# Extra products of the identity on TensorE in the waits at the beginnings and ends of stages

## The reference

```python
x = x + L0_xattn(ln(x), ctx, ctx)      # l0a: 16 heads, softmax over 256 keys
x = x + L0_ffn(ln(x))                  # l0f: mixture of experts, 1 of 8 experts for a token
x = x + L1_xattn(ctx, ln(x))           # dtw: dynamic time warping alignment
x = x + L1_ffn(ln(x))                  # l1f: silu(gate) * up, down
x = x + L2_xattn(ln(x), ctx)           # l2a: attention with rotated q and k
x = x + L2_ffn(ln(x))                  # l2f: mixture of experts, 2 of 8 for a token
x = x + L3_xattn(ln(x), ctx, ctx)      # l3a: attention over the 32 largest scores
x = x + L3_ffn(ln(x))                  # l3g finds token groups, l3f attends within them
```

## Time and profile before

| | us |
|---|---|
| median of 3 runs | 2589.59 (2580.96 to 2591.77) |
| the profiled execution, its own time | 2591.72 |
| its span, first to last instruction | 2589.9 |
| mean granted clock of TensorE | 0.790 of full speed |
| busy: PE, DVE, ACT, POOL | 2011.9, 1664.3, 1115.9, 1012.3 |

### The profile page before, as it was taken

The page is one execution under the profiler, slowest core; times in us unless marked ns, Lnnn a source line. Parts: engine busy times, 40 slices in busy tenths (PEclk is TensorE's granted clock), DMA queues, the critical chain, the costliest instruction groups (busy, mean ns, idle before and its releaser), DMA issues. The chain is left out here.

```text
span 2589.9 us, 40039 instructions
## 1 busy us (share of the span) xinstructions
PE 2011.9 (78%) x13073; PEld 1624.0 (63%) x13073; DVE 1664.3 (64%) x5395; ACT 1115.9 (43%) x3119; POOL 1012.3 (39%) x955
## 2 busy tenths in 40 slices
PE   6985898699559948866999847777777778765996
PEld 4664797699538835555999835555555555544663
DVE  5764111588972258843111189999999999964773
ACT  3552232555221114431333246666666666641443
POOL 3310453200000046403555446666666666606430
PEclk9996899655779979967999966667667666567997
DMA  2111575410210012124464230000000000000112
GB/s 88 65 55 58 215 244 182 121 21 1 81 37 1 0 45 73 57 69 145 136 212 156 80 96 9 1 9 9 1 9 9 1 1 1 1 7 26 42 47 77
DMA packets 91587, 161.09 MB, mean 62 GB/s; under 512 B 18366, under 2 KB 69718, under 8 KB 83414
## 3 DMA queue, kind: packets, MB, share of 16 engines
q0 software_dynamic: 23808, 85.50, 9.6%
q1 hardware_dynamic: 67576, 73.06, 9.0%
HBM read 194.38 MB, written 33.33 MB: 88 GB/s over the span
## 5 line engine op out<-in xcount | busy, mean ns | idle before, releaser
L555 DVE MATCH_REPLACE8 l3a_left<-l3a_top,l3a_left 128x256 f32<-128x256 f32 x768 | 308.9, 410 | 0.0
L548 DVE MAX8 l3a_top<-l3a_left 128x8 f32<-128x256 f32 x768 | 286.0, 415 | 0.0
L365 POOL TENSOR_TENSOR l3a_prob<-l3a_expd,l3a_rest 128x512 f32<-128x512 f32 x128 | 162.5, 1270 | 230.3 <-ACT l3a_rest L445 230.0
L270 PE MATMUL l3a_psT<-all_ident,l3a_prob 128*128 128x128 f32 x512 | 123.5, 387 | 163.9 <-POOL l3a_prob L365 163.9
L288 PE MATMUL l3a_psO<-l3a_probT,l3a_vp 128*128 128x128 f32 x1024 | 216.0, 377 | 28.8 <-ACT l3a_probT L461 28.8
L288 PEld LDWEIGHTS l3a_psO<-l3a_probT,l3a_vp 128*128 128x128 f32 x1024 | 185.5, 271 | 81.7 <-ACT l3a_probT L461 48.3
L270 PEld LDWEIGHTS l3a_psT<-all_ident,l3a_prob 128*128 128x128 f32 x512 | 83.8, 196 | 186.6 <-POOL l3a_prob L365 186.1
L352 POOL TENSOR_TENSOR l3a_kept<-l3a_raw_sc,l3a_mone 128x512 f32<-128x512 f32 x128 | 163.3, 1276 | 49.1 <-ACT l3a_raw_sc L429 48.9
L1465 ACT ACTIVATE l2f_hT<-l2f_psH,l2f_wt 128x128 f32<-128x128 f32 x312 | 89.2, 369 | 216.3 <-PE l2f_psH L1397 216.3
L445 ACT ACTIVATE l3a_rest<-l3a_left,l3a_nmax 128x256 f32<-128x256 f32 x256 | 116.1, 502 | 151.5 <-DVE l3a_left L555 150.8
L932 POOL TENSOR_SCALAR l2a_xn<-all_x,l2a_nmean,all_rstd 128x256 f32<-128x256 f32 x16 | 8.8, 562 | 433.6 <-DVE all_rstd L106 433.6
(11 more groups left out here) (528 smaller groups left out, 4715.5 us busy)
## 6 DMA issues: line engine op xcount, KB each, us to landing
o_at<-l0a_oraw SPq DMA_DIRECT2D x16, 256.0 KB, 2.0
l0a_osum<-o_at SPq DMA_DIRECT2D x32, 128.0 KB
kv_at<-dtw_kv SPq DMA_DIRECT2D x8, 512.0 KB, 2.8
o_at<-l2a_oraw SPq DMA_DIRECT2D x16, 256.0 KB, 2.0
l2a_osum<-o_at SPq DMA_DIRECT2D x32, 128.0 KB
l2f_yb<-rows_y SPq DMA_DIRECT2D x8, 512.0 KB, 7.4
o_at<-l3f_oraw SPq DMA_DIRECT2D x16, 256.0 KB, 2.0
l3f_osum<-o_at SPq DMA_DIRECT2D x32, 128.0 KB
```

The source lines that it names most:

```text
L270: mm = nc.tensor.transpose(psT[u % 2][:, kc, e, :], prob[:, u % 4, e, kc * P:kc * P + P], ident[:])
L365: nc.gpsimd.tensor_tensor(prob[:, u % 4, :, :], expd[:, u % 2, :, :], rest[:, u % 2, :, :], ALU.subtract).then_inc(picked, 1)
L548: ins = nc.vector.max(top[:, e, eight], rows[:, e, :] if r else scores[:, e, :])
L555: ins = nc.vector.match_replace(out=rows[:, e, :], in_to_replace=top[:, e, eight], in_values=rows[:, e, :] if r else scores[:, e, :], imm_ ...
```

## The change

A new helper issues `n` products of the 128 x 128 identity with four copies of itself side by side (512 columns) into a PSUM bank, which the next real product overwrites; nothing reads them and they signal nothing. It is called in four functions, always just before a wait of TensorE: in `paired_attention` before the first `x_norm` (2), before the first `xT_ev` (2), before `scores_1(0)` waits (11 in l2a, 3 in l3f, none in l0a), before `values(15)` (1) and before `out_project(7)` (8); in `moe` before `turn(0)` (4); in `gated_ffn` at the start (2) and after the first transpositions (1); in `find_groups` at the start (1) and before `queries(0)` (3). In `scores_1` the four `take`s also move ahead of the two other waits.

```diff
--- before.py
+++ after.py
@@ -72,6 +72,13 @@
 
     def block(self):
         return self.blocks.enter_context(self.nc.Block())
+
+
+def keep_busy(nc, out, ident, n):
+
+
+    for _ in range(n):
+        nc.tensor.matmul(out, ident[:], ident[:].unsqueeze(1).to_broadcast([P, 4, P]), start=True, stop=True)
 
 
 class RowStats:
@@ -766,8 +773,13 @@
                     mm = nc.tensor.matmul(out, lhs[c], rhs[c], start=(c == 0), stop=(c == DC - 1))
                 return mm
 
+            def busy(out, n):
+                keep_busy(nc, out[:].rearrange("p e n -> p (e n)"), ident, n)
+
             def x_turned(b):
                 out = take("xT", b)
+                if b == 0:
+                    busy(out, 2)
                 pe.wait_ge(x_norm, b + 1)
                 for c in range(DC):
                     for t in range(QT):
@@ -776,6 +788,8 @@
 
             def projected(b, what):
                 out = take(what, b)
+                if b == 0 and what == "q":
+                    busy(out, 2)
                 if what == "q" or not given:
                     pe.wait_ge(xT_ev, b + 1)
                 else:
@@ -792,10 +806,14 @@
 
             def scores_1(n):
                 b, c, qt = n // 4, n % 4 // 2, n % 2
+                out = [take("s1", 4 * n + j) for j in range(4)]
+                if n == 0 and groups is not None:
+                    busy(out[0], 3)
+                if n == 0 and rope is not None:
+                    busy(out[0], 11)
                 if n % 4 == 0:
                     pe.wait_ge(qd_set, b + 1)
                     pe.wait_ge(k2_set, b + 1)
-                out = [take("s1", 4 * n + j) for j in range(4)]
                 for e in (1, 0):
                     for j in range(4):
                         r = slice(32 * j, 32 * j + 32)
@@ -828,6 +846,8 @@
             def values(y):
                 b, c = y // 2, y % 2
                 out = take("pv", y)
+                if y == 2 * B - 1:
+                    busy(out, 1)
                 pe.wait_ge(exp_done, 8 * (y + 1))
                 if c == 0:
                     pe.wait_ge(v_ev, b + 1)
@@ -841,6 +861,8 @@
 
             def out_project(b):
                 out = take("out", b)
+                if b == B - 1:
+                    busy(out, 8)
                 if groups is None:
                     pe.wait_ge(o_set, 2 * (b + 1))
                 else:
@@ -1436,6 +1458,7 @@
                                       start=(n == 0), stop=(n == KT - 1))
             mm.then_inc(turned, 1)
 
+            keep_busy(nc, psX[:], ident, 4)
             turn(0)
             up(0)
             turn(1)
@@ -2104,6 +2127,8 @@
                     for t in range(QT):
                         mm = nc.tensor.transpose(psT[:, c * S + t * P:c * S + t * P + P], xn[:, p, t, c * P:c * P + P], ident[:])
                 mm.then_inc(t_done, 1)
+                if not again:
+                    keep_busy(nc, psG[0][:], ident, 1)
                 pe.wait_ge(t_read, b + 1)
                 if not again:
                     pe.wait_ge(w_set, 1)
@@ -2128,6 +2153,7 @@
                                               start=(f == 0), stop=(f == HC - 1))
                 mm.then_inc(y_ps, 1)
 
+            keep_busy(nc, psG[0][:], ident, 2)
             pe.wait_ge(x_norm, 1)
             up(0, 0, False)
             up(1, 1, True)
@@ -2288,11 +2314,14 @@
                                               start=(c == 0), stop=(c == DC - 1))
                 mm.then_inc(q_ps, 1)
 
+            keep_busy(nc, psQ[0][:].rearrange("p t n -> p (t n)"), ident, 1)
             turn(0)
             pe.wait_ge(w_in, 48)
             for b in range(B):
                 if b + 1 < B:
                     turn(b + 1)
+                if b == 0:
+                    keep_busy(nc, psQ[0][:].rearrange("p t n -> p (t n)"), ident, 3)
                 queries(b)
             pe.wait_ge(c_done, 1)
             nc.tensor.transpose(psF[0:4 * NT, :], col[:].rearrange("p f t -> p (f t)"), ident[:]).then_inc(f_done, 1)
```

## The result

The changed kernel takes 2575.0 us (median of 12 runs, 2559.6 to 2582.4) against 2585.7 us for the kernel before beside it (12 runs, 2579.3 to 2591.8): 10.7 us less, a ratio of 0.9947 with a 95% interval of 0.9932 to 0.9962 (the two medians by themselves give 0.9959). The forecast was 2576, faster. Three executions of this document's kernels lie far above all others of their kernel (5936.0 and 4485.1 us of the kernel before, 2834.5 of the kernel with calls in the body), and no median counts them.

The account below looks back on a forecast made before the run. TensorE's low clock after idle waits was taken to bound stretches where others wait for it. Ten terms sum to 14.2 us (best 22.4, worst about -5): 2577.5 from the profile, 2575.4 on the median's scale, forecast 2576, range 2566 to 2590.

Parts of the forecast that it names:

- l0a beginning: Start of l0a: four calls keep TensorE dense before q, so q and k run fast; gain 2.3 us (0 to 3.1).
- l3f end: End of l3f: eight calls overrun 4.07 us of idle, out_project(7) starts 2.7 to 4.2 late; -1.2 us (-2.4 to -0.9).
- l2f: Expert block l2f: four calls before turn(0) end 0 to 1.6 late, up(0) 3.73 for 6.73; 2.1 us (-0.1 to 3.1).
- l0f: Expert block l0f: calls end before the gather lands, clock probably falls again; 0.6 us (0 to 1.9).
- l1f: l1f: three calls at the start and behind the transpositions, L2118's first eight could win 1.8; 0.9 us (-0.2 to 2.0).
- l2a beginning: Start of l2a: faster q 1.6, eleven calls before scores_1(0) perhaps 2.1 more; taken 2.0 us of 3.7 (0 to 3.7).
- l3g: l3g: three calls about 0.2 late, queries(0) 3.78 to about 2.4; 1.1 us (-0.4 to 1.8).
- l3f beginning: Start of l3f: calls before q delay it, three before scores_1(0) give 1.6 back; net 0.7 us (-2.0 to 1.4).
- The ends of l0a and l2a: values(15) takes 1.93 and moves everything behind it, out_project(7) takes 1.99 for 3.75; 2.8 (0 to 3.0) and 2.9 (0 to 3.4).
- Rival A: Wherever 1.5 us or more of idle stays behind the products the clock falls again; gain 7.4, so 2582 us; chance 0.27.
- Rival B: Identity products don't raise the clock, each costs 1.72 and runs past its wait; 20.7 slower, 2610 us; chance 0.06.
- Rival C: Shifts are swallowed by DVE or POOL later in a stage, only ends pay; 6.6, so 2583 us; chance 0.13.

Follow-up runs that it names:

- the kernel with calls in the body: Changed kernel with waits filled nearer their length, plus seven calls before scores_1(4) of l2a and one before scores_2(28) in l0a and l2a: 2562.4 against 2589.0 us.
- the third profile of before: The kernel before, unaltered, profiled once more after a look that fell into a 5998 us execution: 2587.5 us, one execution.
- the beginnings alone: Changed kernel without the calls before values(15) and out_project(7), all others left: 2574.5 against 2587.4 us of the kernel before, ratio 0.9952.
- the ends alone: Changed kernel with only the calls before values(15) and out_project(7) left: 2584.7 against 2587.4 us of the kernel before, ratio 0.9989.
- the last two kernels: Filled waits and body calls, plus one call before scores_2 per l2a batch from the fourth: 2569.3; that with l3f's end filled: 2566.4; kernel before 2585.6 us.
- thin ones: Changed kernel with each 512-column product replaced by five of 8 columns, every call in its place: 2628.2 against 2587.4 us of the kernel before, ratio 1.0155.
- the second profile of before: The kernel before, unaltered, one look; it fell into an execution of 5998 us with every product about twice its low-clock time.

## Why the prediction was right

Each term measured: the profiles that have the calls against those that have not, where a stage's calls are the same. A beginning is the time from the stage's first instruction (of DVE, in l0a) to its first add_out (DVE, all_x from a bank), an end that from the sixth add_out to the eighth; the others are whole stages, start to start. The row from which the first comes, in the changed kernel (92.72 - 12.77 = 80.0, one of the seven behind the 80.1; the same in the first profile of before gives 83.2):

```profile
92.72 0.69 DVE L1199 TENSOR_TENSOR all_x<-l0a_bank,all_x 128x512 f32<-128x512 f32 x1 [0.97 <-PE l0a_bank L773]
```

```
term              forecast   measured   profiles without / with the calls
l0a beginning       2.3        2.3      82.4 (3) / 80.1 (7)
l0a end             2.8        1.5      23.9 (3) / 22.4 (5)
l2a end             2.9        1.7      23.5 (3) / 21.8 (5)
l3f end            -1.2       -2.0      out_project(6) to (7) 7.4 (4) / 11.1 (4), 1.7 back
l2f                 2.1        2.5      364.7 (3) / 362.2 (5)
l0f                 0.6        0.0      236.5 (3) / 236.5 (5)
l1f                 0.9        1.3      150.6 (3) / 149.3 (5)
l2a beginning       2.0        2.6      102.4 (3) / 99.8 (4)
l3g                 1.1        2.5      43.2 (3) / 40.7 (5)
l3f beginning       0.7        0.2      104.9 (3) / 104.7 (4)
sum                14.2       12.6      medians of the runs: 10.7, and again 10.1
```

By the spread of the single profiles the means carry an error of 0.5 to 1 us each, l3f's beginning more; the sum agrees with the times of the runs within what ten such errors add up to.

**That 2576 met 2575.0 to 1 us is luck.** The sum was taken from the median of three runs of before, 2589.6; the twelve beside the changed kernel have 2585.7. From there 14.2 less is 2571.5. The base was 3.9 too high and the gain, against the medians, 3.5 too high, and the two cancel. Within the sum the ends, l0f and l3f's beginning were put too high, l2f, l1f, l2a's beginning and l3g too low.

**The mechanism** was right: the new products cost 0.44 an instruction at the high level, they raise the clock (3.7 us behind the first of them in l0f and in l2f, by the clock records of the changed kernel's trace), and where it then holds, the work behind them takes its mid-stage time. The signs that I named came: values(15) at 1.93 in all three stages, up(0) of l2f at 3.84, out_project(7) of l3f late with no idle before it.

**L0a's beginning, l2f, l1f and l2a's beginning** stand within 0.6 of their terms. In l2a the total is right, its parts are not settled. I took half of what the eleven calls could give for the risk of the 2.7 us that they leave; of the four profiles that have them, scores_1(0) was slow in one (2.09), nearly fast in one (1.25) and fast in two. But the slow one has one of the early add_outs (at 99.3 us) and the nearly fast one the late one (101.5). The first q, which I took at 1.99, took that in the changed kernel's first profile alone and 2.89 to 3.78 in the four others with the same two calls before it.

**The ends of l0a and l2a were over-sized**, 1.5 and 1.7 for 2.8 and 2.9, and this is the step that failed: that values "takes 1.93 as in mid-stage instead of 3.10 and 3.50, and everything behind it moves: 1.2 and 1.6". It does not move. From values(15) to out_project(7) it is 13.9 us with values at 3.10 (before), 13.9 at 1.93 (the changed kernel, and the third profile of before), 14.7 at 3.61 and again at 1.93; in l2a 14.2 and 13.7 slow, and 13.5 to 14.0 fast in seven profiles, 14.4, 14.8 and 15.7 in three. The trip through memory takes the shift back. Its store of o_at and the load behind it, in the changed kernel (values 1.93), then in the kernel with the beginnings alone (values 3.61), l0a:

```profile
195.64 0.32 SPq L717 DMA_DIRECT2D o_at<-l0a_oraw  x1
...
198.85 1.07 SPq L723 DMA_DIRECT2D l0a_osum<-o_at  x2
```

```profile
200.48 0.32 SPq L717 DMA_DIRECT2D o_at<-l0a_oraw  x1
...
202.54 1.07 SPq L723 DMA_DIRECT2D l0a_osum<-o_at  x2
```

The store goes out 2.6 us behind values(15)'s start in the one and 4.3 in the other, the load 5.8 and 6.3: 3.2 us from store to load where values is fast, 2.1 where it is slow. By the program the load waits for the store to land, and in the traces it goes out 0.02 us behind that, so it is the store itself that takes longer. A fast values sends it out while the loads of the result before, issued at -0.2 and +0.4 us from values(15)'s start, are still under way (DVE starts on them at 5.3); behind a slow values it meets only their end (5.0). So the store runs beside them and gains little. That the two get in each other's way is read from these times; no run varies it. What pays at the ends is mostly out_project(7), and that by luck: in the five profiles with eight calls it took 1.99 five times, behind 2.8 to 3.2 of idle, and 2.8 to 3.5 the other five, behind 2.8 to 3.8. The idle left is longer than the 1.5 to 2 that I took for the same reason: out_project(6) ends earlier and out_project(7) doesn't start earlier.

**L3g was under-sized**: 1.1 for 2.5, outside of my bounds. I thought the three calls would run at the low level past the wait. The clock rose in time in all five profiles, queries(0) took 1.99 for 3.78, and all of the 1.8 came through. Most of the rest is the write of the flags to the next stage's first row, 4.65 us in the profile of before and 3.16 in that of the ends alone, which has no calls there either; this was the draw.

**L3f's end** cost 2.0, inside the bounds. What I had not seen is that it can be filled: calls before out_project(6), then three and not eight, turn the loss into 1.8 to 2.5 gained. **L3f's beginning** gave nothing that can be seen. Of the four profiles scores_1(0) was slow in three, behind 2.6 of idle (first add_out at 104.8 to 105.5), and fast in one (103.5). Without the calls before q the mean of five profiles is 104.2, 0.7 better than with none at all, but those three lie between 103.7 and 105.9, so this is not shown.

**Rival A**, that any rest of 1.5 us or more loses the clock, was half right: such a rest sometimes loses it and sometimes not, even at 3.2. Values(15) shows it best. With one call before it, which leaves 1.08, it took 1.93 in all 23 rows of the profiles; without, behind 2.23, it was fast in 2 of 13 and took 2.60 to 3.62 in the others. But 1.5 us is no border either: in the last two kernels the clock fell at a scores_2 of l2a behind 1.19 and 1.10 of idle (1.79 and 1.75). **Rival B** needs products that don't count for the clock: thin ones don't, these do. **Rival C** fell with the beginnings alone, though in l3f's beginning something like it may be so.

**The 20 us between the two profiles** are 12.6 of the change and the rest of bodies: 4.0 in l0a's body alone, where before lost the clock once (values 3.39 at 188.25) and the changed one did not. In the other profiles without a call there, it was lost in three and held in five. What remained unsettled is what decides whether a rest loses the clock, whether calls in the body pay, what the eleven calls of l2a give by themselves, and whether l3f's calls before q cost anything.

## What to carry to other kernels

Where TensorE waits behind an idle stretch and is itself what the next engines wait for, full-width products into a bank that is already its own buy the high clock back at no cost that these runs show, as long as they end before the wait does. Count them so that about 1 us of idle or less stays: before values(15) the clock held 23 times of 23 at 1.1, and 2 times of 13 at 2.2. That is a better chance and no guarantee, since elsewhere it fell behind 1.1 and 1.2, and from 1.6 to 3.8 it was luck; each 0.86 us call past the wait is lost outright. Price each place on its own: the one place that was clearly overrun cost 2.0 us, more than an end of the changed kernel gave, and the four calls that did nothing in l0f were worth 2.5 us once doubled. Read the trace for which instruction the wait stands before: two scores_2 off, a call fills nothing. And one profile of each kernel can't be subtracted where single rests move a batch by 1.6 to 3 us.

## What the runs showed of the hardware

- **Short rests are a lottery.** The same row behind the same 1.67 us of idle ran at 1.15 or at 2.09, in one profile at 2.09 three batches running, in most slow in one batch of four. I had expected a length of the rest that decides. What decides instead, no run here separates.
- **Busy is not enough.** Back-to-back 8-column products let the clock fall to the low level within 3 us and kept it there for 11 (mean 0.90, then 0.50). The Trainium skill (TensorE: Matmul & The Clock Gate, Part 4: PE-mode transpose) sets apart transpose-mode work as not counting for the clock; here ordinary products did not count either, when they were narrow.
- **A granted clock of 1.00 can stand for no record.** The window of the first products says 1.00, while four instructions of 512 columns take 3.75, the low level's time. The trace of the changed kernel holds no clock record before 17.3 us, and the view counts time without one as full clock:

```profile
12.80:16.40 3.60, 3.60 (x5) 1.10 (x5) 3.37 (x16) 1.68 (x3) 1.16 (x3) 1.00 0.46 106
```

- **One execution with TensorE at a quarter.** In the second profile of before, the products took about four times their high-level time, eight of 256 columns 6.7 to 6.9 us, over the whole span of 5996 us; DVE, ACT and POOL kept their busy times (1669, 1114 and 1012 us). Its trace has no clock record at all, so the 1.00 that its windows show says nothing. Three more executions were far too long, without a trace: 5936 us with a mean granted clock of 0.286, 2834.5 us with 0.669 and 4485 us with 1.00. The first two fit a TensorE that was slow for the whole of the time or a part. I have no cause for it.

```profile
27.62 6.88 PE L766 MATMUL l0a_bank<-l0a_kvT,l0a_wk 128*128 128x256 f32 x8
```
